# Layer norm ahead of the experts taken by token, expert weights centred on the chip, and a reordered end of the program

## The chip, the cores and the metric

The kernel runs on one core of a Trainium2 chip. The metric is the device time of one execution in microseconds (us); less is better. The engines are named as in the profile: PE is TensorE, DVE is VectorE, ACT is ScalarE, POOL is GpSimd, SP is SyncE, whose queue issues most DMAs.

## The reference

Four sequences (batches) of 256 tokens, width 128, go through four residual steps. `ctx` is a context of 4 x 1601 tokens. All is float32.

```python
x = x + xattn0(layernorm(x), ctx)          # 16 heads of 8, rotary, bias by distance, gate
x = x + tanh(layernorm(x) @ W1 @ W2 @ W3 + b)
x = x + xattn1(layernorm(x), ctx, mask)    # 16 heads of 8
x = x + experts(layernorm(x))
...
def experts(x):                            # E = 8 experts, K = 2
    scores = maximum(x @ gate_W + gate_b, 1e-4)
    p = softmax(scores)
    w = maximum(p, 0.1); w = w / (sum of w over the two largest p)
    comb = where(one of the two largest, w, 0)
    y = einsum('bsd,edf->bsef', x, expert_W) + expert_b
    return einsum('bsef,bse->bsf', y, comb) / 2
```

## The kernel before, in words

**Stages and units.** The program has NJ = 8 stages j. Stages 0 to 3 do the first attention for batches 0 to 3, stages 4 to 7 the second. A stage has UB = 52 units: 13 tiles of 124 (the last 113) context tokens times 4 groups of 4 heads. For each unit PE makes the scores (L414, in the first attention also a bias, L408) into two PSUM banks, ACT takes their exponential (L941), and PE multiplies that by the values (L430), accumulating in banks ACC and ACC+1. The loop goes by pairs of units: PE issues the scores of the next pair, then `beside(j, 2 * pair)`, then the values of this pair, then `beside(j, 2 * pair + 1)`.

**Slots.** `beside(j, slot)` holds all other PE work: it is placed by slot numbers, 0 to 51 in a stage. Slot 3 picks the attention's sums of the stage before (`pick`); `gate_at` places the steps that end a batch of the first attention, `expert_at` those of the experts. In stages 5, 6 and 7 the nine steps of `experts(j - 5, k)` stand at slots 8, 10, 11, 13, 14, 24, 25, 27 and 30; for the last batch they follow the last stage. Work in an even slot stands ahead of the values of its pair, work in an odd slot behind them.

**Side banks.** All of this side work shares two PSUM banks, LOW = 6 and HIGH = 7. `fill(bank, ...)` numbers every filling and makes PE wait until DVE or ACT has read the filling before (`seen`); PE's queue is in order, so such a wait also holds the scores and values behind it.

**The end of an attention.** `copy_sums(j)` (L1268) takes the sums out of PSUM. `pick(j)` (L442) brings numerators into LOW and denominators into HIGH, `take_sums` (L1273) copies them, and `finish` tests the denominators, takes their reciprocal (L1282), multiplies (L1285, which raises `batch_done`), tests the result and reduces the tests into `checks` (L1290). `decide()` reduces all `checks` to the flag `redo`, which decides at the end of the program whether everything is computed again in a safe way.

**The norm ahead of the experts** works with features on partitions. `project` adds the attention's output to x (L1362); PE takes the mean (L466); DVE subtracts it and squares (L1310, L1312); PE sums the squares (L472); DVE adds eps (L1316); POOL raises to the power -0.5 (L870); PE spreads the result over the partitions (L479); DVE multiplies (L1321). Then PE makes the gate scores (L523), `choose` (L1375 to L1411, 18 small DVE instructions with one ACT exponential, L956, among them) makes the factors `comb`, PE turns them (L530), makes x plus the experts' biases (L536, L538) into LOW, and makes the experts' products for 128 tokens at a time, four experts into LOW and four into HIGH (L545). `weigh` adds each product times its factor to y (L1427, 16 instructions of 128 x 128 per batch). One `dma_start` per 128 tokens stores y (L728).

**Other queues.** `query_parts(b)` splits the second attention's queries into three bf16 parts on DVE (L1355, L1357) and POOL. POOL norms the context of batch 3 (`norm_context`, L835) after `query_parts(0)`; PE's keys of batch 3 (L352, stage 2, slot 7) wait for that. In stage 1 `fold_weights` fills LOW at slot 4 and HIGH at slot 5, `turn_rstd` fills HIGH at slot 6 of stages 1 and 2. SP's queue stores and places keys in order of the program; ACT's `second_keys` (L967) waits for such a store before it overwrites its buffer.

## Time and profile before

| | before |
|---|---|
| median of 3 runs | 655.69 us (654.56 to 656.54) |
| the profiled execution, its own time | 653.17 us |
| its span, first to last instruction | 651.4 us |
| mean granted TensorE clock | 0.939 |
| PE, DVE, ACT, POOL busy | 86%, 43%, 66%, 22% of the span |

The stages begin (start of their first exponential) at 42.55, 149.20, 234.08, 317.92, 379.95, 435.59, 493.85 and 551.99 us; the last exponential ends at 609.7 us. The span is what the profile's rows lie in; the execution's own time is 1.8 us more. An engine's idle time costs something only where another engine on the path waits for it, so each part of the program is to be read by which wait ends last in it. "[0.52 <-PE ps L414]" behind a row says that its engine was idle for 0.52 us before it, and what ended that.

### The profile page before, as it was taken

How to read it: one execution, taken by the hardware profiler on the slowest of the kernel's cores; microseconds unless marked ns; L12 is line 12 of the kernel's file. 1: busy time of each engine (PE TensorE's matmuls, PEld its weight loads, DVE VectorE, ACT ScalarE, POOL GpSimd, SP SyncE). 2: the span in 40 equal slices, each digit the busy share in tenths (PEclk: the TensorE clock that was granted, in tenths of full speed). 3: DMA queues.
4: the chain of work that ended last, by engine and by line, in shares of the span. 5: the costliest groups of instructions: out<-in, count | busy, mean ns of one | idle time of the engine just before them, and what ended most of it. 6: DMA issues, size and time to landing. Idle time of an engine off the chain costs nothing.

```text
span 651.4 us, 15145 instructions
## 1 busy us (share of the span) xinstructions
PE 561.3 (86%) x6326; PEld 278.2 (43%) x6326; DVE 277.1 (43%) x711; ACT 431.1 (66%) x486; POOL 142.4 (22%) x149
## 2 busy tenths in 40 slices
PE   4665896999979996999999999999999999999643
PEld 3432453545434553445555445434443443443231
DVE  5732742483754424544242243134344343433333
ACT  1224554866747773777778897998789869888400
POOL 5552622354436003541011000100000000000000
PEclk9867997999979997999999999999999999999856
DMA  6366264438755700445370066039016501000000
GB/s 166 94 186 178 71 218 168 104 115 243 226 157 146 264 26 5 138 130 179 83 189 28 27 147 141 27 82 230 4 46 144 133 10 53 2 1 10 1 0 12
DMA packets 54185, 68.12 MB, mean 105 GB/s; under 512 B 13347, under 2 KB 45551, under 8 KB 54112
## 3 DMA queue, kind: packets, MB, share of 16 engines
q1 hardware_dynamic: 50528, 59.29, 32.8%
q0 software_dynamic: 1280, 6.56, 3.4%
q10 hardware_dynamic: 2304, 1.25, 0.7%
q8 instruction: 51, 0.84, 0.5%
q14 instruction: 22, 0.18, 0.1%
HBM read 35.20 MB, written 18.83 MB: 83 GB/s over the span
## 4 chain that ended last, share of the span: by engine, by line
PE 53%; issue 14%; ACT 10%; SPq 7%; DMA 7%; DVE 7%; POOL 1%; ACTq 0%; POOLq 0%; DVEq 0%
PE ps L430 19%; PE ps L414 10%; ACT probs L941 8%; PE ps L408 7%; DMA k_scratch<-k_parts 4%; PE ps L360 4%; SPq L676 2%; PE ps L545 2%; SPq L699 1%; DMA ctx_tokens<-in_ctx 1%; PE ps L352 1%; PE ps L479 1%; PE ps L466 1%; DMA mask_q<-in_mask 1%; PE ps L472 1%
## 5 line engine op out<-in xcount | busy, mean ns | idle before, releaser
L941 ACT ACTIVATE probs<-ps 124x1024 f32<-124x1024 f32 (+1 forms) x416 | 399.8, 1024 | 110.7 <-PE ps L414 109.0
L430 PE MATMUL ps<-probs,values 124*9 124x256 f32 (+1 forms) x3328 | 221.4, 384 | 1.4 <-DVE out_sums L1268 1.3
L414 PE MATMUL ps<-q_side,k_side 63*124 63x256 bf16 (+1 forms) x1664 | 164.5, 283 | 13.0 <-ACT probs L941 11.2
L414 PEld LDWEIGHTS ps<-q_side,k_side 63*124 63x124 bf16 (+1 forms) x1664 | 98.1, 133 | 88.4 <-ACT probs L941 58.7
L430 PEld LDWEIGHTS ps<-probs,values 124*9 124x9 f32 (+1 forms) x3328 | 71.0, 90 | 94.1 <-issue 40.5
L408 PE MATMUL ps<-bias_g,bias_w 64*124 64x512 bf16 (+1 forms) x416 | 88.0, 419 | 25.5 <-ACT probs L941 22.0
L408 PEld LDWEIGHTS ps<-bias_g,bias_w 64*124 64x124 bf16 (+1 forms) x416 | 28.1, 131 | 69.3 <-ACT probs L941 45.3
L870 POOL TENSOR_TENSOR post_rstd<-post_rstd,power 128x2 f32<-128x2 f32 x12 | 8.4, 704 | 167.0 <-DVE post_rstd L1316 167.0
L967 ACT ACTIVATE k<-ps,columns_sb 128x496 f32<-128x496 f32 (+2 forms) x16 | 9.5, 594 | 48.2 <-PE ps L354 30.4
L1188 DVE SCALAR_TENSOR_TENSOR k_swapped<-ps,beta_products,k_sin_sb 32x496 f32<-32x496 f32 (+2 forms) x64 | 40.4, 631 | 0.9
L829 POOL DMA_DIRECT2D mask_q<-in_mask x16 | 9.1, 570 | 141.4 <-DVE checks L1247 141.4
L1254 DVE TENSOR_REDUCE sample_max<-ps 128x8 f32<-128x512 f32 x32 | 20.6, 686 | 41.3 <-PE ps L377 41.3
L1230 DVE TENSOR_TENSOR values<-ps,rstd 124x256 f32<-124x256 f32 (+2 forms) x32 | 12.0, 374 | 60.6 <-PE ps L360 60.5
L360 PE MATMUL ps<-w_centred,ctx_turned 128*124 128x256 f32 (+1 forms) x104 | 32.9, 439 | 4.8 <-ACT k_parts L968 2.5
L1427 DVE SCALAR_TENSOR_TENSOR y<-ps,comb,y 128x128 f32<-128x128 f32 x64 | 22.4, 351 | 16.7 <-PE ps L545 14.7
L360 PEld LDWEIGHTS ps<-w_centred,ctx_turned 128*124 128x124 f32 (+1 forms) x104 | 18.6, 202 | 16.4 <-issue 8.0
L1247 DVE TENSOR_REDUCE checks<-mask_q 128x1 f32<-128x801 int32 (+1 forms) x16 | 15.6, 977 | 23.0 <-DMA mask_q<-in_mask 22.9
L855 POOL TENSOR_TENSOR k<-k,k_parts 128x496 f32<-128x496 f32 (+2 forms) x16 | 15.1, 944 | 42.0 <-ACT k_parts L968 41.9
L352 PE MATMUL ps<-ctx_normed,w_centred 128*128 128x496 f32 (+2 forms) x32 | 16.9, 613 | 8.3 <-POOL ctx_normed L835 5.7
L859 POOL TENSOR_TENSOR k<-k,k_parts 128x496 f32<-128x496 f32 (+2 forms) x16 | 15.1, 944 | 29.5 <-DVE k_parts L1199 28.3
L1268 DVE COPY out_sums<-ps 128x512 f32<-128x512 f32 x16 | 10.6, 686 | 23.6 <-PE ps L430 23.6
L545 PE MATMUL ps<-expert_w_sb,xn 128*128 128x512 f32 x32 | 18.8, 718 | 0.6 <-DVE y L1420 0.6
(190 smaller groups left out, 481.6 us busy)
## 6 DMA issues: line engine op xcount, KB each, us to landing
k_side<-k_scratch SPq DMA_DIRECT2D x24, 400.2 KB, 9.0
k_side<-k_parts SPq DMA_DIRECT2D x48, 124.0 KB, 2.4
k_scratch<-k_parts SPq DMA_DIRECT2D x16, 372.0 KB, 4.1
v_scratch<-values SPq DMA_DIRECT2D x4, 936.0 KB, 8.1
values<-v_scratch SPq DMA_DIRECT2D x4, 936.0 KB, 14.4
v_scratch<-v SPq DMA_DIRECT2D x12, 288.0 KB, 3.4
mask_q<-in_mask POOLq DMA_DIRECT2D x8, 400.5 KB, 3.9
mask_q<-in_mask POOLq DMA_DIRECT2D x8, 400.0 KB, 3.5
```

The lines of the kernel that those rows point to most:

```text
L352: pe.matmul(ps[:, LOW, 0:w], w0c[:, 2, :], cn[:, k_0:k_1], start=True, stop=True).then_inc(made[LOW], 1)
L360: last = pe.matmul(ps[0:r, bank, 2 * D * i:2 * D * i + 2 * D], ct[:, TS * t:TS * t + r], wvv.rearrange("p l d -> p (l d)"), start=True, st ...
L408: pe.matmul(ps[0:width, bank, :], G["bias_w"][rows, at], G["bias_g"][rows, t:t + 1, :].broadcast_to((HALF, 2, SQ)), start=True, stop=False ...
L414: last = pe.matmul(ps[0:width, bank, SQ * i:SQ * (i + 1)], kst[rows, j % 2, 2 * g + i, at], qst[rows, j % 2, 2 * g + i, :], start=not bias ...
L430: last = pe.matmul(ps[32 * i:32 * i + VC, ACC + g // 2, SQ * (g % 2):SQ * (g % 2) + SQ], v[0:rows, j % 2, t, h, :], p[0:rows, u % 4, SQ * ...
L545: pe.matmul(ps[:, bank, :], xn[:, b * SQ + 128 * t:b * SQ + 128 * t + 128], ew[:, 4 * i:4 * i + 4, :].rearrange("p e d -> p (e d)"), start ...
L855: pool.tensor_tensor(k1[:, s, 0:w], k1[:, s, 0:w], kp1[:, s, 0, 0:w], ALU.subtract).then_inc(rest1, 1)
L941: act.activation(p[0:rows, u % 4, :], ps[0:rows, s:s + 2, :].rearrange("p a n -> p (a n)"), ACT.Exp)\
L1188: last = dve.scalar_tensor_tensor(out=kb[to:to + 32, 0:w], in0=ps[at:at + 32, LOW, 0:w], scalar=beta_cols[at:at + 32, 2:3], in1=k_sin[at:a ...
L1247: dve.tensor_reduce(checks[:, at:at + 1], mask_q[:, 0:k_1 - k_0], AX.X, ALU.min, apply_absolute_value=True)\
L1254: dve.tensor_reduce(mx[:, c, H8 * half_:H8 * half_ + H8], ps[:, bank, :].rearrange("p (h k) -> p h k", k=SAMPLE), AX.X, ALU.max).then_inc( ...
L1427: add = dve.scalar_tensor_tensor(out=out[:, t, :], in0=ps[:, bank, D * i:D * i + D], scalar=comb[:, t, e:e + 1], in1=out[:, t, :], op0=ALU ...
```

## The change

1. **By token.** `project` only adds. Step 1 of the experts transposes x with a matmul against the identity into HIGH and multiplies x by the gate weights into LOW, both without a norm before them. `token_norm` takes mean and variance along the free axis (`bn_stats`, `bn_aggr`), POOL raises to the power, and the result, one number per token, is a factor on the gate scores and on `comb` (`comb_rstd`). The copy of the transposed x is y's start; the mean, sum of squares, spread and normed x are gone. 
2. **Centred weights.** Since the products take x and not x less its mean, `centre_experts` multiplies gate and expert weights by the centring matrix once, at slot 24 of stage 4: three matmuls on PE, three copies on DVE.
3. **Slots.** Six steps in place of nine, at slots 8, 10, 22, 24, 26 and 29. The gate's exponential on ACT stands 7 units behind slot 10 (before: 7 behind slot 14).
4. **End of each attention.** `take_sums` takes the reciprocal of the denominators directly from PSUM, copies them, and multiplies the numerators from PSUM; the tests (`check_sums`) come after. LOW and HIGH are released later, `batch_done` is raised earlier.
5. **End of the program.** The last batch's products are made ahead of `comb`, for both halves of the tokens, into banks 0 to 3. DVE weighs the first half in 8 steps; ACT scales the second half's 8 products, and DVE adds them in three halving steps and one more. `check_sums` stands between `token_norm` and `choose`, `decide` last.
6. `w_scaled` lies in a part of `probs` and no longer in a tile of its own.

```diff
+CENTRE_EXPERTS_AT = (NB, 24)
 def expert_at(j, slot):
-    steps = (8, 10, 11, 13, 14, 24, 25, 27, 30)
+    steps = (8, 10, 22, 24, 26, 29)
...
-        GATE_STEPS = 17
+        GATE_STEPS = 18
...
+            def centre_experts():
+                pe.wait_ge(expert_in, 16 * N_EXPERT)
+                fill(LOW, "gate_w")
+                pe.matmul(ps[:, LOW, 0:E], centre[:], gw[:], start=True, stop=True).then_inc(made[LOW], 1)
+                for i, bank in enumerate((HIGH, LOW)):
+                    fill(bank, "expert_w", i)
+                    pe.matmul(ps[:, bank, :], centre[:], ew[:, 4 * i:4 * i + 4, :].rearrange("p e d -> p (e d)"), start=True, stop=True)\
+                      .then_inc(made[bank], 1)
...
                 elif k == 1:
                     pe.wait_ge(seen[LOW], side.of(LOW, "o1", b))
-                    post_mean(HIGH, ("mean", norm), b)
-                elif k == 2:
-                    post_var(LOW, ("var", norm), norm)
-                elif k == 3:
-                    post_spread(HIGH, ("spread", norm), norm)
-                elif k == 4:
-                    pe.wait_ge(seen[HIGH], side.of(HIGH, "spread", norm))
...
+                    fill(HIGH, "xt", b)
+                    for t in range(TT):
+                        last = pe.matmul(ps[:, HIGH, 128 * t:128 * t + 128], x[:, b * SQ + 128 * t:b * SQ + 128 * t + 128], ident[:],
+                                         start=True, stop=True)
+                    last.then_inc(made[HIGH], 1)
+                    pe.wait_ge(gw_centred, 1)
                     fill(LOW, "gate", b)
...
             pick(NJ - 1)
-            for k in range(4):
+            for k in range(2):
+                experts(NB - 1, k)
+            for t in range(TT):
+                expert(NB - 1, t, (2 * t, 2 * t + 1))
+            for k in (2, 3):
                 experts(NB - 1, k)
             pe.wait_ge(least_ready, 1)
-            fill(LOW, "least")
-            pe.transpose(ps[0:1, LOW, 0:128], least[:], ident[:]).then_inc(made[LOW], 1)
-            for k in range(4, 9):
-                experts(NB - 1, k)
+            fill(HIGH, "least")
+            pe.transpose(ps[0:1, HIGH, 0:128], least[:], ident[:]).then_inc(made[HIGH], 1)
...
             def take_sums(j):
-                for out, bank in ((num, LOW), (den, HIGH)):
-                    dve.wait_ge(made[bank], side.of(bank, "pick", j))
-                    dve.tensor_copy(out[:], ps[:, bank, 0:SQ]).then_inc(seen[bank], 1)
+                dve.wait_ge(made[HIGH], side.of(HIGH, "pick", j))
+                dve.reciprocal(inv[:], ps[:, HIGH, 0:SQ]).then_inc(den_ready, 1)
+                dve.tensor_copy(den[:], ps[:, HIGH, 0:SQ]).then_inc(seen[HIGH], 1)
+                dve.wait_ge(made[LOW], side.of(LOW, "pick", j))
+                dve.wait_ge(den_ready, j + 1)
+                dve.tensor_tensor(att[:, columns(j % NB)], ps[:, LOW, 0:SQ], inv[:], ALU.mult).then_inc(seen[LOW], 1)
+                dve.wait_ge(seen[LOW], side.of(LOW, "pick", j))
+                dve.sem_inc(batch_done, 1)
...
+            def token_norm(b):
+                dve.wait_ge(made[HIGH], side.of(HIGH, "xt", b))
+                for t in range(TT):
+                    dve.bn_stats(est[:, t, :], ps[:, HIGH, 128 * t:128 * t + 128]).then_inc(e_stats, 1)
+                dve.wait_ge(e_stats, TT * (b + 1))
+                for t in range(TT):
+                    dve.bn_aggr(emv[:, t, :], est[:, t, :]).then_inc(e_aggr, 1)
+                dve.wait_ge(e_aggr, TT * (b + 1))
+                dve.tensor_scalar(prs[:], emv[:, :, 1], EPS, None, ALU.add).then_inc(e_var, 1)
...
+                dve.tensor_copy(y[:, b % 2], ps[:, HIGH, 0:SQ].rearrange("p (t d) -> p t d", d=D)).then_inc(seen[HIGH], 1)
...
+            def weigh_last():
...
+                for e in range(E):
+                    dve.wait_ge(last_made, 1 + e // 4)
+                    dve.scalar_tensor_tensor(out=out[:, 0, :], in0=ps[:, e // 4, D * (e % 4):D * (e % 4) + D], scalar=comb_r[:, 0, e:e + 1],
+                                             in1=out[:, 0, :], op0=ALU.mult, op1=ALU.add).then_inc(y_done if e == E - 1 else last_sum, 1)
...
+                for i, n in enumerate((4 * D, 2 * D, D)):
+                    dve.tensor_tensor(weighed[:, 0:n], weighed[:, 0:n], weighed[:, n:2 * n], ALU.add).then_inc(last_sum, 1)
+                    dve.wait_ge(last_sum, E + i)
+                dve.tensor_tensor(out[:, 1, :], out[:, 1, :], weighed[:, 0:D], ALU.add).then_inc(y_done, 1)
...
             take_sums(NJ - 1)
-            finish(NJ - 1)
             project(NB - 1)
+            token_norm(NB - 1)
+            check_sums(NJ - 1)
+            choose(NB - 1)
+            weigh_last()
             decide()
-            choose(NB - 1)
-            weigh(NB - 1)
```

Where the order of the work moves, it is shown here as the program issues it, before and now.

PE, the end of the program (behind the last values), before:

```order
924 L442 MATMUL ps<-out_sums,pick 32x256 x8
925 L510 MATMUL ps<-att,L_wo_sb 128x256
926 L466 MATMUL ps<-x,ones_mean 128x256
927 L472 MATMUL ps<-ones_mean,post 128x1 x2
928 L479 MATMUL ps<-ident,post_rstd 128x128 x2
929 L620 MATMUL ps<-ident,least 1x128
930 L523 MATMUL ps<-gate_w_sb,xn 128x8 x2
931 L530 MATMUL ps<-ident,comb 8x128 x2
932 L536 MATMUL ps<-ident,x 128x128
933 L538 MATMUL ps<-expert_b_sb,comb_t 128x128
936 L545 MATMUL ps<-expert_w_sb,xn 128x512 x4
```

and now:

```order
911 L449 MATMUL ps<-out_sums,pick 32x256 x8
912 L532 MATMUL ps<-att,L_wo_sb 128x256
913 L537 MATMUL ps<-ident,x 128x128 x2
914 L543 MATMUL ps<-gate_w_sb,x 128x8 x2
915 L523 MATMUL ps<-expert_w_sb,x 128x512 x4
916 L550 MATMUL ps<-ident,comb 8x128 x2
917 L556 MATMUL ps<-expert_b_sb,comb_t 128x128 x2
918 L640 MATMUL ps<-ident,least 1x128
```

The four products (x4) now stand ahead of the turned factors, the norm's three steps are gone, and the flag's transpose is last.

DVE, stage 2 behind the copies of the attention's sums, up to the query parts (`CAST`) for which POOL waits, before:

```order
201 L1273 COPY num<-ps 128x256
202 L1273 COPY den<-ps 128x256
203 L1170 COPY rstd<-ps 124x13
204 L1277 TENSOR_SCALAR inside<-den 128x256
205 L1279 SCALAR_TENSOR_TENSOR inside<-den,inside 128x256
206 L1282 RECIPROCAL den<-den 128x256
207 L1285 TENSOR_TENSOR att<-num,den 128x256
208 L1287 SCALAR_TENSOR_TENSOR inside<-att,inside 128x256
209 L1290 TENSOR_REDUCE checks<-inside 128x1
210 L1355 CAST q_parts<-post 128x256
211 L1357 CAST q_parts<-post 128x256
```

and now:

```order
200 L1298 RECIPROCAL inverse<-ps 128x256
201 L1299 COPY den<-ps 128x256
202 L1302 TENSOR_TENSOR att<-ps,inverse 128x256
203 L1196 COPY rstd<-ps 124x13
204 L1308 TENSOR_SCALAR inside<-den 128x256
205 L1310 SCALAR_TENSOR_TENSOR inside<-den,inside 128x256
206 L1313 SCALAR_TENSOR_TENSOR inside<-att,inside 128x256
207 L1316 TENSOR_REDUCE checks<-inside 128x1
208 L1381 CAST q_parts<-post 128x256
209 L1383 CAST q_parts<-post 128x256
```

Reciprocal and product now stand ahead of the copy of `rstd` (which waits for PE's step at slot 6), the tests behind it.

## Rows read from the trace of the kernel before

**Rows 1.** The page, part 1: busy us, share of the span, instructions

```profile
PE 561.3 (86%) x6326; PEld 278.2 (43%) x6326; DVE 277.1 (43%) x711; ACT 431.1 (66%) x486; POOL 142.4 (22%) x149
```

**Rows 2.** Stretches: us, busy us (count) of PE, PEld, DVE, ACT, POOL, granted clock, DMA share, GB/s

```profile
541.00:575.00 34.00, 32.06 (x434) 14.49 (x426) 11.15 (x23) 31.02 (x34) 1.26 (x2) 1.00 0.05 14
251.00:255.00 4.00, 3.75 (x24) 2.38 (x28) 1.72 (x5) 2.06 (x4) 4.00 (x5) 0.50 0.02 4
638.40:640.80 2.40, 2.40 (x4) 1.01 (x4) 1.62 (x5) 0.00 (x0) 0.00 (x0) 0.50 0.00 0
```

**Rows 3.** Timeline of the end: start us, us, engine line op tiles [idle before]

```profile
611.16 1.07 PE L442 MATMUL ps<-out_sums,pick 128*32 128x256 f32 x16 [0.81 <-DVE out_sums L1268]
...
612.30 0.42 DVE L1273 COPY den<-ps 128x256 f32<-128x256 f32 x1
612.76 0.29 DVE L1277 TENSOR_SCALAR inside<-den 128x256 bf16<-128x256 f32 x1
...
613.55 1.75 DVE L1282 RECIPROCAL den<-den 128x256 f32<-128x256 f32 x1
...
615.82 1.22 PE L510 MATMUL ps<-att,L_wo_sb 128*128 128x256 f32 x2 [3.58 <-DVE att L1285]
...
617.08 0.48 DVE L1362 SCALAR_TENSOR_TENSOR x<-ps,folded_bias,x 128x256 f32<-128x256 f32 x1 [0.40 <-PE ps L510]
...
621.85 1.22 PE L479 MATMUL ps<-ident,post_rstd 128*128 128x128 f32 x4 [1.02 <-POOL post_rstd L870]
...
624.51 1.00 PE L523 MATMUL ps<-gate_w_sb,xn 128*128 128x8 f32 x4 [0.46 <-DVE lowest L1441]
625.54 0.17 DVE L1375 TENSOR_TENSOR gate_scores<-ps,gate_b_sb 128x16 f32<-128x16 f32 x1 [1.00 <-PE ps L523]
...
630.00 0.59 PE L530 MATMUL ps<-ident,comb 128*8 128x128 f32 x2 [4.49 <-DVE comb L1411]
...
631.82 0.79 PE L538 MATMUL ps<-expert_b_sb,comb_t 8*128 8x128 f32 x2
...
634.64 6.91 PE L545 MATMUL ps<-expert_w_sb,xn 128*128 128x512 f32 x8 [0.59 <-DVE y L1420]
...
640.58 3.06 DVE L1427 SCALAR_TENSOR_TENSOR y<-ps,comb,y 128x128 f32<-128x128 f32 x8 [0.54 <-PE ps L545]
```

**Rows 4.** The statistics of x's tokens near the program's start: ns min/median/max

```profile
L1058 DVE BATCH_NORM_STATS2 x_stats<-out_sums x8: 275/278/289, 5.0 to 66.4; 128x6 f32<-128x128 f32 x8
```

**Rows 5.** Timeline of stage 6: exponentials behind side work, and the side work

```profile
506.63 1.94 ACT L941 ACTIVATE probs<-ps 124x1024 f32<-124x1024 f32 x2 [0.52 <-PE ps L414]
509.42 1.94 ACT L941 ACTIVATE probs<-ps 124x1024 f32<-124x1024 f32 x2 [0.85 <-PE ps L414]
511.62 1.94 ACT L941 ACTIVATE probs<-ps 124x1024 f32<-124x1024 f32 x2 [0.26 <-PE ps L414]
513.76 3.77 ACT L941 ACTIVATE probs<-ps 124x1024 f32<-124x1024 f32 x4 [0.21 <-PE ps L414]
517.39 0.24 ACT L956 ACTIVATE gate_p<-gate_scores 128x16 f32<-128x16 f32 x1
...
525.19 1.94 ACT L941 ACTIVATE probs<-ps 124x1024 f32<-124x1024 f32 x2 [1.87 <-PE ps L414]
...
526.27 1.98 PE L545 MATMUL ps<-expert_w_sb,xn 128*128 128x512 f32 x4
...
528.66 3.77 ACT L941 ACTIVATE probs<-ps 124x1024 f32<-124x1024 f32 x4 [1.54 <-PE ps L414]
534.38 3.77 ACT L941 ACTIVATE probs<-ps 124x1024 f32<-124x1024 f32 x4 [1.95 <-PE ps L414]
```

**Rows 6.** Timelines of stages 1 and 2

```profile
186.04 0.67 ACT L967 ACTIVATE k<-ps,columns_sb 128x496 f32<-128x496 f32 x1 [3.96 <-DMA k_scratch<-k_parts]
...
244.65 0.17 DVE L1170 COPY rstd<-ps 124x13 f32<-124x13 f32 x1 [2.96 <-PE ps L344]
...
251.25 0.79 PE L352 MATMUL ps<-ctx_normed,w_centred 128*128 128x124 f32 x2 [5.66 <-POOL ctx_normed L835]
```

129 lines of the change are left out of this document (81 added, 48 removed).

## The prediction

> **What bounds the kernel now.** I first read part 1 of the page [rows 1]: PE is busy for 86% of the span, ACT for 66%. That says where to look and not what anything is worth, so I went on by stretches [rows 2]: in an undisturbed part of the last stages PE is busy for 32.06 of 34 us and ACT for 31.02, at the full clock (2.4 GHz). Both are nearly full, so PE work beside the units turns up as idle time of ACT. The timeline of stage 6 shows that [rows 5]: seven of its idle gaps lie behind the experts' steps, 0.52, 0.85, 0.26, 0.21, 1.87, 1.54 and 1.95 us, together 7.20 us. The third view is the timeline behind the last exponential [rows 3]. There only one thing happens at a time: from PE's pick at 611.16 to the end of the last weighing step at 643.64 each row begins where another ends, for 32.5 us, and every saved wait is saved time. PE runs there at half rate (1.2 GHz), still in 638.40 to 640.80 [rows 2]; before the clock fell it had gone idle with the last scores. The last view is the timelines of stages 1 and 2 [rows 6], for what the change to `take_sums` meets: in stage 2 PE stands 5.66 us for POOL's normed context, which waits for DVE.
>
> **The end of the program**, step by step, from the same 611.16 us [rows 3]. Denominators are picked at 611.16 + 1.07 = 612.23. Reciprocal 1.75, copy 0.42 and product 0.42, with some 0.2 of gaps, raise `batch_done` in time for PE at 615.05 (before 615.82): 0.8 won, since three tests and a copy no longer stand ahead. PE's output step to DVE's start takes 617.08 - 615.82 = 1.26, DVE's addition 0.48, a gap 0.06: 616.85. Then, in place of mean, square, variance, power, spread and multiply (each a PE or DVE step of its own, up to the gate's matmuls at 624.51), comes the transposed x, four matmul instructions like the spread's, 1.26 to DVE's start: 618.11. Statistics twice 0.28 [rows 4]; aggregates and the addition of eps at most 0.5 (three small instructions, each no longer than the 0.17 of such rows): 619.2. POOL's power now runs beside DVE's copy to y and the four tests: 0.42 + 0.29 + 0.43 + 0.42 + 0.42 and gaps, 2.2 us, and these decide: `choose` starts at 621.4. It ended, with PE's next start, 630.00 - 625.54 = 4.46 later; one more small instruction makes 4.6: factors at 626.0. Meanwhile PE has made the gate's scores (1.0, to 619.1) and the products, 6.91, to 626.05: both arrive together. Turning the factors 0.6, their copy 0.42 as for any 256 elements, the biases two of the four matmuls, 1.5 at half rate, to 628.65. DVE adds them, 0.45, weighs eight products, 3.06 + 0.05, to 632.2. The second half is ACT's: a scaled copy of 128 x 128 can't take less than the 0.24 of its smallest row [rows 5], and I allow 0.5, so at most 4 us from 626.2, ready by 630.2, under DVE's eight. Four additions of 512, 256, 128 and 128 elements: the 256-element rows take 0.42, the others scaled by it 0.7, 0.29 and 0.29, with gaps 1.85: 634.05 against 643.64. **9.6 us saved.** The flag, 1.1 us of work moved behind it, lies beside the storing of y, which took from 643.64 to the end of the span at 651.4 with what follows; if nothing covered it, it would cost 1.1.
>
> The half rate may end sooner. PE now works without a gap from 616.85 to 626.05, 9.2 us; before, some 9 us of biases and products (631.82 to 640.80) passed and the clock was still at half at their end. So the rise would meet only the last steps: turned factors and biases, 2.1 us at half rate, half of that at most saved. Between 0 and 1.1 I take **0.5**.
>
> **Stages 5 to 7.** I price steps by the idle gap they left in ACT [rows 5], not by their own length. The output step stays (0.52). Transposed x and gate stand in one pair, as mean and variance did: 0.85 again. The spread's and the old gate's slots are empty: 0.26 + 0.21 saved. The pair with turned factors and four matmuls for x and biases left 1.87; now the factors stand alone (0.2, as the short steps did) and two matmuls two slots on (0.5). The products [rows 5] left 1.54 and 1.95; in an even and an odd slot with work in the pair before, 1.62 and 1.54. Sum now 0.52 + 0.85 + 0.2 + 0.5 + 1.62 + 1.54 = 5.2 against 7.2: 2.0 a stage, **5.9 us** for three. The centring adds, in stage 4, two products of the same 512 columns in an even slot, 1.95, and a small one: **2.1 us lost.** Net 3.8. Bounds: if only the two empty slots help, 3 x 0.47 - 2.1 = 0.7 is lost; if the new slots hid the biases and factors whole, 3 x 2.7 - 2.1 = 6.0 is won. I stay near the middle, since every step has a row of its kind.
>
> What makes this hold is that nobody waits for the factors. ACT's small exponential started at 517.39, behind 21 units; now it stands four units sooner, near 513.0. The scores will be ready for it by then: slot 10's work lies ahead of the exponential at 509.42, transposed x is there by 507.4; 1.1 to the statistics' end, POOL's power 0.9 at most, DVE's small steps 0.9, 510.3. The factors follow 3.5 us later, 516.5. Slot 22 lies 12 units behind slot 10 (506.7), at 1.05 us a unit 519.2. The slack is 2.7 us.
>
> **`take_sums` in the other stages.** In stage 2 DVE stood idle for 2.96 us between its two copies and the copy of `rstd` [rows 6]; reciprocal and product now fill that, and the query parts come 1.75 + 0.42 + gaps = 2.2 us sooner. POOL and PE's keys (251.25) wait for just that, so PE starts at 249.0. But the clock was at half there [rows 2], after 5.66 us of idle PE, and PE was full (3.75 of 4 us). If it stays at half as long, work started 2.2 us sooner is worth half: **1.1 us**; 0 if another wait takes over, 4 if the shorter wait spares the fall. In stage 1 the same edit costs: LOW is released 1.8 us later than `fold_weights` at slot 4 wants it, and PE's queue stands. I cost this at nothing, because ACT later waits 3.96 us for a store of keys at 186.04 [rows 6], a chain through SP's queue of stores that this PE work doesn't feed; without that cover it is 1.8. In stages 3 to 7 `batch_done` comes sooner, but PE had no wait of note there: nothing. `w_scaled` within `probs` moves nothing.
>
> One price has no row: a reciprocal that reads PSUM. The row from SBUF says 1.75 for 256 elements, 7 ns each; a copy from PSUM takes 0.42 and a scalar test from SBUF 0.29 [rows 3], so the source makes 0.13 of difference there. The lower end is 1.75, the upper 3.5 (twice), and I take 1.75, since 7 ns per element is far above the 1.6 of the copy.
>
> The Trainium skill has a rule against this edit ("VectorE: DVE Perf Modes", "Why PSUM operands drop a tier"): an operand in PSUM excludes the mode in which both SBUF read ports serve one tensor. The rows of copy and test agree in kind. For the reciprocal the rule would give up to the doubled time, the second rival below.
>
> **Sum.** 9.6 + 0.5 + 3.8 + 1.1 = 15.0 us. The profiled execution took 653.17, so 638.2 for its like; it lay 2.5 below the median of the runs shown, 655.69, and against that I forecast **640.7**.
>
> **The rivals.**
> - *The gaps don't close* (0.10). The slots move the work but PE is as full, and stage 1's stall isn't covered: the stages give nothing, -1.8 beside: 9.6 + 0.5 + 1.1 - 1.8 = 9.4, so 646.3. For it: PE busy 94% there. Against: ACT's gaps follow PE's side work row by row.
> - *The reciprocal from PSUM is twice as long* (0.08). 1.75 more at the end; in stage 2 it overruns DVE's idle time by 1.0: 15.0 - 2.8 = 12.2, so 643.5. Against: 7 ns per element.
> - *The clock is kinder* (0.09). It doesn't fall in stage 2 (3 more) and rises early at the end (0.6 more): 18.6, so 637.1. For it: PE's wait in stage 2 shrinks to 3.5 us.
> - *Slower* (0.03). The factors come too late for slot 22 in each of stages 5 to 7: PE stands ahead of the values, ACT runs dry and the clock falls to half as it did in stage 2. With 5 us of wait and 6 us at half rate (3 lost) that is 8 a stage, 24 in all: 655.7 - 15.0 + 24 = 664.7. It turns the sign once the wait costs over 5 us a stage, that is, when ACT's exponential or POOL's power comes 4 to 8 us later than worked out above. Against: 2.7 us of slack.
> - *No change* (0.02): the stored y or the flag sets the end and the stages lose what they gain, 655.7.
>
> **How the numbers follow.** The forecast's own case has 0.68. About 2 us (0.3%) is what a measurement of this kernel tells from no change. All cases but the last two are faster: 0.95, same 0.02, slower 0.03. The range: from between the forecast and the kind clock, 636.0, to between the doubled reciprocal and the first rival, 645.5; that leaves out the first rival and the last two, 0.15, and a little of the others.
>
> **What would show it right or wrong.** At the end: the reciprocal from PSUM near 1.75 us; `choose` starting some 10 us behind the pick and waiting for nothing; products ending as the factors arrive; the last addition some 23 us behind the pick (before 32.5). ACT's idle time in stages 5 to 7 near 6.4 us each, in stage 4 some 2 us more than before. PE's wait for the normed context near 3.5 us. Wrong would be a wait of PE for the factors at slot 22, an exponential of the gate behind an idle ACT, a stage 1 that is 2 us longer, or ACT's scaled copies ending after DVE's eighth step.

## The result, and the profile after

| | before | changed |
|---|---|---|
| median (lowest to highest of 4 runs each) | 655.82 us (654.56 to 656.54) | 637.00 us (634.12 to 637.61) |
| ratio | | 0.971, 95% interval 0.967 to 0.974 |
| the profiled execution, and its span | 653.17, 651.4 us | 636.57, 634.5 us |
| mean granted TensorE clock | 0.939 | 0.942 |

The change saves 18.8 us, 3.7 us more than the 15.0 that were forecast; 640.7 was predicted, and 637.0 lies 1.0 us inside the range's lower end, 636.0.

Where it went is read stage by stage. A stage's length is the time from its first exponential to that of the next stage (of stage 7, to the end of its last exponential); "start" is the first exponential of all, "end" runs from the start of PE's last pick to the end of the last instruction that adds to y. The second column is a further profile of the kernel before, the last one of a further run of the changed kernel (both are among the experiments).

| us | before | before, again | changed | changed, again |
|---|---|---|---|---|
| start | 42.55 | 43.49 | 42.47 | 42.84 |
| stage 0 | 106.65 | 109.93 | 108.80 | 109.33 |
| stage 1 | 84.89 | 85.39 | 84.32 | 83.31 |
| stage 2 | 83.83 | 83.96 | 82.61 | 82.07 |
| stage 3 | 62.03 | 62.03 | 62.02 | 62.03 |
| stage 4 | 55.64 | 55.64 | 57.78 | 57.78 |
| stages 5, 6, 7 | 58.26, 58.13, 57.69 | 58.33, 58.13, 57.69 | 55.95, 55.82, 55.24 | 55.98, 55.82, 55.24 |
| end | 32.48 | 31.79 | 20.40 | 20.49 |

By the first profile of each, the end gave 12.1, stages 5 to 7 gave 7.1, stage 2 gave 1.2, stage 1 0.6, and stage 4 took 2.1: 18.9 together. Stage 0, which the change does not touch, came out 2.1 us longer in this one profile. Stages 0 and 1 vary by some 3 us from profile to profile, whatever the kernel; that is why the two profiled executions lie only 16.6 us apart and the medians 18.8. Both stages wait for stores of keys, and their length goes with the time that the clock is at half rate in them (experiment 8). Stages 3 to 7 repeat to 0.2 us, so one profile is enough there.

The page, part 1 (busy us, share of the span, instructions), against [rows 1]:

```profile
PE 549.7 (87%) x6292; PEld 271.3 (43%) x6292; DVE 272.1 (43%) x718; ACT 433.1 (68%) x494; POOL 142.4 (22%) x149
```

PE lost 11.6 us of work and its share of the span rose. The shares say nothing of the gain; the stretches do. Stretches of the changed kernel (us, then busy us and count of PE, PEld, DVE, ACT, POOL, granted clock, DMA share, GB/s), the first of them in stage 2, the rest at the end of the program:

```profile
251.00:255.00 4.00, 4.00 (x32) 2.04 (x31) 1.72 (x5) 2.56 (x4) 3.78 (x5) 0.50 0.01 4
606.50:611.50 5.00, 1.84 (x19) 0.82 (x20) 2.85 (x4) 0.00 (x0) 0.00 (x0) 1.00 0.00 0
611.50:618.30 6.80, 6.80 (x15) 3.70 (x16) 5.01 (x22) 0.22 (x1) 0.69 (x1) 0.50 0.01 4
618.30:621.70 3.40, 2.13 (x9) 0.82 (x7) 1.99 (x11) 1.52 (x7) 0.00 (x0) 0.99 0.00 0
```

In stage 2 the clock still fell to half (1.2 GHz), as in [rows 2]. At the end it fell 5.0 us behind the pick, over the transposed x and the products, and was full again (2.4 GHz) from 618.3. Before, it had fallen 2.3 us behind the pick and stayed down for 27.3 us, until 640.8, so for all of PE's steps but the last 0.75 us of the products.

The timeline of the end (start us, us, engine line operation tiles, idle before and what ended it), against [rows 3]:

```profile
606.50 1.07 PE L449 MATMUL ps<-out_sums,pick 128*32 128x256 f32 x16 [0.81 <-DVE out_sums L1294]
607.63 1.76 DVE L1298 RECIPROCAL inverse<-ps 128x256 f32<-128x256 f32 x1 [1.19 <-PE ps L449]
...
610.14 0.67 PE L532 MATMUL ps<-att,L_wo_sb 128*128 128x256 f32 x2 [2.58 <-DVEq L1304]
...
611.39 1.14 PE L537 MATMUL ps<-ident,x 128*128 128x128 f32 x4 [0.58 <-DVE x L1388]
...
612.57 0.49 DVE L1395 BATCH_NORM_STATS2 e_stats<-ps 128x6 f32<-128x128 f32 x2 [1.23 <-PE ps L537]
613.03 6.31 PE L523 MATMUL ps<-expert_w_sb,x 128*128 128x512 f32 x8
613.10 0.25 DVE L1398 BATCH_NORM_AGGREGATE e_mean_var<-e_stats 128x2 f32<-128x6 f32 x2
...
613.63 0.69 POOL L891 TENSOR_TENSOR post_rstd<-post_rstd,power 128x2 f32<-128x2 f32 x1 [48.45 <-DVE post_rstd L1400]
...
615.36 0.35 DVE L1424 SCALAR_TENSOR_TENSOR gate_scores<-ps,post_rstd,gate_b_sb 128x8 f32<-128x8 f32 x2
...
619.99 0.38 PE L550 MATMUL ps<-ident,comb 128*8 128x128 f32 x2 [0.65 <-DVE comb L1461]
620.18 2.18 ACT L1072 ACTIVATE probs<-ps,comb_rstd 128x128 f32<-128x128 f32 x8 [3.60 <-DVE comb_rstd L1463]
...
620.87 0.71 PE L556 MATMUL ps<-expert_b_sb,comb_t 8*128 8x128 f32 x4 [0.50 <-DVE comb_t L1465]
621.69 0.42 DVE L1471 TENSOR_TENSOR y<-y,ps 128x256 f32<-128x256 f32 x1 [0.87 <-PE ps L556]
622.14 3.06 DVE L1499 SCALAR_TENSOR_TENSOR y<-ps,comb_rstd,y 128x128 f32<-128x128 f32 x8
625.11 1.47 DVE L1506 TENSOR_TENSOR probs<-probs 128x512 f32<-128x512 f32 x3
...
626.61 0.29 DVE L1508 TENSOR_TENSOR y<-y,probs 128x128 f32<-128x128 f32 x1
```

The reader is to see that from 612.57 on DVE goes from step to step, with short waits only for ACT's exponential, the turned factors and the biases: the products, 6.31 us of PE, end at 619.3, ahead of the factors at 619.99, and nobody waits for them. ACT's copies end at 622.4, long before DVE needs them at 625.11. The reciprocal from PSUM took 1.76 us, as from SBUF. The flag, now worked out behind y, is ready 21.4 us behind the pick, and from the last addition to the end of the span it is 7.6 us (before 7.7): its 1.1 us of work is covered.

Stage 6, exponentials behind side work, and the two steps that depend on the gate, against [rows 5]:

```profile
506.73 1.94 ACT L962 ACTIVATE probs<-ps 124x1024 f32<-124x1024 f32 x2 [0.52 <-PE ps L421]
509.28 3.77 ACT L962 ACTIVATE probs<-ps 124x1024 f32<-124x1024 f32 x4 [0.61 <-PE ps L421]
512.91 0.24 ACT L977 ACTIVATE gate_p<-gate_scores 128x16 f32<-128x16 f32 x1
521.01 1.94 ACT L962 ACTIVATE probs<-ps 124x1024 f32<-124x1024 f32 x2 [0.35 <-PE ps L421]
523.21 1.94 ACT L962 ACTIVATE probs<-ps 124x1024 f32<-124x1024 f32 x2 [0.26 <-PE ps L421]
526.73 1.94 ACT L962 ACTIVATE probs<-ps 124x1024 f32<-124x1024 f32 x2 [1.58 <-PE ps L421]
530.20 11.62 ACT L962 ACTIVATE probs<-ps 124x1024 f32<-124x1024 f32 x12 [1.54 <-PE ps L421]
```

```profile
519.24 0.38 PE L550 MATMUL ps<-ident,comb 128*8 128x128 f32 x2
```

Six gaps, together 4.86 us, where seven made 7.20. The gate's exponential starts without an idle ACT ahead of it, at 512.91 (forecast 513.0), and PE turns the factors at 519.24 without a wait.

Stage 2 (DVE's reciprocal and PE's keys), against [rows 6]:

```profile
242.77 1.76 DVE L1298 RECIPROCAL inverse<-ps 128x256 f32<-128x256 f32 x1 [4.41 <-PE ps L449]
...
250.50 0.79 PE L359 MATMUL ps<-ctx_normed,w_centred 128*128 128x124 f32 x2 [3.41 <-POOL ctx_normed L856]
```

PE waits 3.41 us for the normed context and not 5.66, 2.25 less, as forecast (near 3.5).

### The profile page after: what moved, and what is told of

It is laid out like the page before. It is cut to its first block, busy times and chain, and to the rows that moved or that the text cites. A ratio compares the mean times of both kernels' runs of the same rounds, so it can differ in the third digit from the quotient of the medians.

```text
span 634.5 us, 15118 instructions
## 1 busy us (share of the span) xinstructions
PE 549.7 (87%) x6292; PEld 271.3 (43%) x6292; DVE 272.1 (43%) x718; ACT 433.1 (68%) x494; POOL 142.4 (22%) x149
## 4 chain that ended last, share of the span: by engine, by line
PE 59%; ACT 12%; DVE 8%; DMA 8%; issue 7%; SPq 4%; ACTq 0%; POOL 0%; DVEq 0%; POOLq 0%
PE ps L437 22%; PE ps L421 12%; ACT probs L962 10%; PE ps L415 8%; DMA k_scratch<-k_parts 5%; PE ps L367 4%; PE ps L523 2%; SPq L694 2%; PE ps L359 1%; DMA ctx_tokens<-in_ctx 1%; PE ps L361 1%; PE ps L449 1%; DMA mask_q<-in_mask 1%; ACT k_parts L989 1%; DVE k_swapped L1214 1%
## 5 line engine op out<-in xcount | busy, mean ns | idle before, releaser
L415 PE MATMUL ps<-bias_g,bias_w 64*124 64x512 bf16 (+1 forms) x416 | 87.8, 418 | 27.6 <-ACT probs L962 24.1
L367 PE MATMUL ps<-w_centred,ctx_turned 128*124 128x256 f32 (+1 forms) x104 | 34.5, 457 | 3.5 <-ACT k_parts L989 2.1
L1298 DVE RECIPROCAL inverse<-ps 128x256 f32<-128x256 f32 x8 | 14.1, 1758 | 28.6 <-PE ps L449 28.6
L359 PE MATMUL ps<-ctx_normed,w_centred 128*128 128x496 f32 (+2 forms) x32 | 16.6, 603 | 6.5 <-POOL ctx_normed L856 3.4
L1483 DVE SCALAR_TENSOR_TENSOR y<-ps,comb_rstd,y 128x128 f32<-128x128 f32 x48 | 16.8, 351 | 12.4 <-PE ps L523 10.9
```

What stands on the lines that cost most here:

```text
L359: pe.matmul(ps[:, LOW, 0:w], w0c[:, 2, :], cn[:, k_0:k_1], start=True, stop=True).then_inc(made[LOW], 1)
L367: last = pe.matmul(ps[0:r, bank, 2 * D * i:2 * D * i + 2 * D], ct[:, TS * t:TS * t + r], wvv.rearrange("p l d -> p (l d)"), start=True, st ...
L415: pe.matmul(ps[0:width, bank, :], G["bias_w"][rows, at], G["bias_g"][rows, t:t + 1, :].broadcast_to((HALF, 2, SQ)), start=True, stop=False ...
L1483: add = dve.scalar_tensor_tensor(out=out[:, t, :], in0=ps[:, bank, D * i:D * i + D], scalar=comb_r[:, t, e:e + 1], in1=out[:, t, :], op0=A ...
```

## The experiments

Each result is the median with the lowest and highest run, and the ratio to the kernel before on the same chip, with its 95% interval. The first four were made together (before: 654.78 us), the next four together (before: 655.05), the last four together (before: 654.75).

**1. The changed kernel again.** No edit.

> The changed kernel once more. The profile after shows 16.9 us less span than the one before: stages 5 to 7 give 7.1, the end behind the pick 12.1, stage 2 1.2, stage 1 0.6, stage 4 takes 2.1, and stage 0 was 2.1 us longer. Theory A: all but stage 0 is the change's own, and stage 0 varies from run to run, so the median lies 18 to 20 us below the kernel before. Theory B: the 3.7 us beyond the forecast come from a lucky phase of PE's clock in that run; then this comes out 15 to 16 us below. In the profile A wants the end (pick to last addition of y) at 20.4 us, give or take 1 for where the half rate begins; B wants 22 to 23.

636.0 us (633.2 to 638.4), ratio 0.971 (0.968 to 0.974), 18.8 us below the kernel before, and the end is 20.49 us: theory A. The size of the gain holds in a second set of runs, and so do the lengths of stages 2 to 7 (table above).

**2. The end in the old order.** The products go back behind the gate, two banks at a time, and DVE weighs all of them. ACT's half of the weighing goes with the order, so this edit tests the two together.

```diff
-            for k in range(2):
-                experts(NB - 1, k)
-            for t in range(TT):
-                expert(NB - 1, t, (2 * t, 2 * t + 1))
-            for k in (2, 3):
+            for k in range(6):
                 experts(NB - 1, k)
...
-            weigh_last()
+            weigh(NB - 1)
```

> Only the order of the end is undone: the last batch's products come behind the factors and biases, into the side banks, and DVE weighs all 16; the norm by token, the centring, the slots and the sums stay. Theory A (the products' 6.3 us lay beside the choice of experts, and ACT took half of the weighing): from the start of the products to the last step of y is then 9.0 us as before, and this starts 15.2 us behind the pick, 24.2 in place of 20.4, with up to 0.9 more for biases at half rate: 3.8 to 4.7 us slower than the changed kernel. Theory B (the factors were the bound, ACT's help is worth nothing): 1 us slower at most.

641.38 us (640.02 to 644.46), ratio 0.981 (0.978 to 0.984): 5.4 us above the changed kernel. The timeline of its end:

```profile
602.80 1.07 PE L449 MATMUL ps<-out_sums,pick 128*32 128x256 f32 x16 [0.81 <-DVE out_sums L1282]
...
619.79 3.78 PE L523 MATMUL ps<-expert_w_sb,x 128*128 128x512 f32 x4 [0.58 <-DVE y L1459]
...
625.34 3.60 PE L523 MATMUL ps<-expert_w_sb,x 128*128 128x512 f32 x4 [1.76 <-DVE y L1471]
627.49 3.06 DVE L1471 SCALAR_TENSOR_TENSOR y<-ps,comb_rstd,y 128x128 f32<-128x128 f32 x8 [2.30 <-PE ps L523]
```

The last addition ends 27.75 us behind the pick, against 20.4. So 7.3 us of the end hang on the products' place and on ACT's help in this form; the medians show 5.4, and what made up for 1.9 us is not shown. This undo costs more than the old end did: here both banks of a half are filled before either is counted as free, so that PE stands 1.76 us between the halves, and products and weighing took 10.8 us where they took 9.0 before (634.64 to 643.64). Less that 1.8, the changed kernel's end is 5.6 us shorter. Of these 0.6 lie ahead of `choose` (it starts 9.5 us behind the pick here, 8.9 in the changed kernel), where the clock had fallen sooner in this profile; 0.7 are turned factors and biases, at half rate here and at the full clock in the changed kernel; 4.3 are the products' place and ACT's half of the weighing, which no run separates. The other 6.5 of the 12.1 lie between the kernel before and this one, both at half rate: `choose` starts 4.9 us sooner (norm by token, earlier sums), and from there to the products it is 1.6 us less, with two of the four matmuls for x and biases gone. My expectation had left the wait between the halves out.

**3. The new sums alone.** The kernel before with the new `take_sums` and `check_sums`, and `w_scaled` within `probs`; nothing else of the change.

```diff
 def take_sums(j):
-    for out, bank in ((num, LOW), (den, HIGH)):
...
+    dve.reciprocal(inv[:], ps[:, HIGH, 0:SQ]).then_inc(den_ready, 1)
...
```

> The kernel before with the new take_sums and check_sums alone (and w_scaled within probs); at the end the tests follow the sums at once. Theory A: stage 2 is 1.1 to 1.2 us shorter, because POOL's context norm starts sooner and half of that is given back at half rate; stage 1's stall of PE at slot 4 (some 1.8 us) is covered by ACT's wait for the store of keys; the end gains 0.4. Sum 1.6 us faster than before. Theory B (the stall of stage 1 counts): 0 to 0.3 us slower than before, and stage 1 1.8 us longer in the profile.

650.43 us (649.2 to 654.8), ratio 0.995 (0.993 to 0.997), 3.5 to 4.4 us below the kernel before, more than was expected. Its profile:

```profile
250.43 0.79 PE L353 MATMUL ps<-ctx_normed,w_centred 128*128 128x124 f32 x2 [3.41 <-POOL ctx_normed L836]
```

Stage 2 is 82.11 us, 1.7 shorter, with the same 3.41 us of wait as in the changed kernel, and the end is 31.25 us, 0.5 to 1.2 shorter: 2.2 to 2.9 us have a place. Stage 1 measured 84.00, not longer. That is within the spread of stage 1, so the last 1 to 2 us of this median are not accounted for; the interval's lower bound, 2.1 us, is met by what the profile shows.

**4. Without the centring.** Its three matmuls and three copies are left out.

```diff
-                if (j, slot) == CENTRE_EXPERTS_AT:
-                    centre_experts()
```

> The changed kernel without the centring of gate and expert weights (that part of the computation is left out). Theory A: the centring costs stage 4 what one idle gap of ACT shows, 2.1 to 2.2 us, and nothing later: this kernel is 2.1 us faster than the changed one, and stage 4 as long as before (55.6 us). Theory B (later stages had made up for it, or the DVE copies hid it): no difference.

633.89 us (631.88 to 635.78), ratio 0.969 (0.966 to 0.971): 2.1 us below the changed kernel (experiment 1), and stage 4 is 55.65 us where it was 57.78. The stage shows the term to its tenth; the medians alone, with runs that spread over 4 us, would not. The gap that the centring leaves in the changed kernel's ACT is this row,

```profile
414.63 10.70 ACT L962 ACTIVATE probs<-ps 124x1024 f32<-124x1024 f32 x11 [2.17 <-PE ps L421]
```

and there is none at this place without it.

**5. Stage 1's banks free at once.** At the start of stage 1 only, DVE copies both sums first as before and divides after `rstd`'s copy.

```diff
-                take_sums(j - 1)
+                copy_first(0) if j == 1 else take_sums(j - 1)
...
                 copy_turned_rstd(j + 1)
+                if j == 1:
+                    divide(0)
```

> The changed kernel, but in stage 1 alone numerators and denominators are copied out first, as before, and reciprocal and product follow behind the folded weights. PE's stall at slot 4 (3.39 us of ACT idle there against 1.79 before) goes. Theory A (covered by ACT's wait for the store of keys, 20 units later): the gap at slot 4 is 1.8 again, the wait for the store is longer by as much, and the time is that of the changed kernel within 1 us. Theory B (not covered): 1.6 us faster.

637.41 us (633.12 to 640.74), ratio 0.972 (0.968 to 0.975), no difference from the changed kernel. ACT's rows in stage 1 show why; first the changed kernel, then this one:

```profile
165.56 1.94 ACT L962 ACTIVATE probs<-ps 124x1024 f32<-124x1024 f32 x2 [3.39 <-PE ps L421]
...
188.45 0.67 ACT L988 ACTIVATE k<-ps,columns_sb 128x496 f32<-128x496 f32 x1 [3.16 <-DMA k_scratch<-k_parts]
```

```profile
165.60 1.94 ACT L962 ACTIVATE probs<-ps 124x1024 f32<-124x1024 f32 x2 [1.79 <-PE ps L421]
...
190.48 0.67 ACT L988 ACTIVATE k<-ps,columns_sb 128x496 f32<-128x496 f32 x1 [5.16 <-DMA k_scratch<-k_parts]
```

The stall of PE is there, 3.39 against 1.79 us, as costed. Taken away, the 1.6 us come back in front of the store, 5.16 against 3.16; the keys behind the store start 37.6 us into the stage here and 37.2 to 37.8 in three profiles of the changed kernel. The cover named in the prediction holds up to there. Behind it the two differ: the clock is at half for 6.8 us of this stage 1, and the stage takes 85.73 us (experiment 8). The changed kernel was not run on this chip; by the ratios to the kernel before (0.972 here, 0.971, 0.971 and 0.974 there) no difference shows.

**6. The six steps at old slots.** 24, 25, 27 and 30 in place of 22, 24, 26 and 29.

```diff
-    steps = (8, 10, 22, 24, 26, 29)
+    steps = (8, 10, 24, 25, 27, 30)
```

> The changed kernel with its last four steps in the old slots: 8, 10, 24, 25, 27, 30 in place of 8, 10, 22, 24, 26, 29. The work is the same, only two steps fall into one pair and the products into an odd and an even slot. Theory A (what a pair's slack takes in decides): gaps of 0.52, 0.61, 1.1 (factors and biases together), 1.54 and 1.95, sum 5.7 against 4.87, so 0.85 a stage and 2.6 us in all slower than the changed kernel. Theory B (only the amount of work on PE counts): no difference.

638.05 us (636.91 to 639.56), ratio 0.974 (0.971 to 0.977). Stages 5 to 7 are 56.39, 56.33 and 55.89 us, 0.44, 0.51 and 0.65 longer, 1.6 in all where 2.6 was expected. PE's busy time in stage 6 is only 0.1 us more (52.55 against 52.44), so neither theory holds alone. Most of what the stages gained is from the work that is gone, and 1.6 of the 7.1 from where the rest stands.

**7. The tests later.** All of the last attention's tests go behind the gate's factors.

```diff
-            check_sums(NJ - 1)
             choose(NB - 1)
+            check_den(NJ - 1)
             weigh_last()
+            check_att(NJ - 1)
             decide()
```

> The changed kernel, at the end with the four tests out of the way of choose: the two tests of the denominators while DVE waits for the biases' matmuls (0.87 us idle), the other two behind y, ahead of the flag. Theory A (the tests are what choose waits for, POOL's power is done 1.0 us sooner): choose starts 1.0 us sooner, the flag comes 0.1 us sooner to 0.2 us later and stays hidden beside the last store: 0.9 to 1.0 us faster. Theory B (products or flag take over as the bound): 0 to 0.3 faster.

634.43 us (633.01 to 636.44), ratio 0.969 (0.966 to 0.972). The chain now goes over POOL's power and not over DVE's tests:

```profile
610.86 0.69 POOL L891 TENSOR_TENSOR post_rstd<-post_rstd,power 128x2 f32<-128x2 f32 x1 [48.54 <-DVE post_rstd L1406]
611.66 0.36 DVE L1430 SCALAR_TENSOR_TENSOR gate_scores<-ps,post_rstd,gate_b_sb 128x8 f32<-128x8 f32 x2 [0.55 <-POOL post_rstd L891]
...
624.99 0.14 DVE L1523 TENSOR_SCALAR redo<-lowest 1x1 int32<-1x1 f32 x1
```

`choose` starts 8.0 us behind the pick (before this edit 8.9) and the last addition ends at 19.57 (20.40). That is about the 0.9 expected. But the flag, with two tests ahead of it, is ready no sooner, 21.5 against 21.4 us behind the pick, and of the 0.9 only 0.2 to 0.5 are left from pick to the end of the span (27.6 us against 28.0, 27.9 and 27.8 in three profiles of the changed kernel). That the flag holds the end is a guess that fits; no run tests it. The median lies 1.6 us below experiment 1, which ran on another chip: more than the profile can account for, and within the scatter of both.

**8. The kernel before again**, one run.

> The kernel before once more, for its stages. Stage 0 was 106.65 us and stage 1 84.89 in the first profile, against 106.6 to 109.3 and 82.4 to 84.8 in five profiles with other ends. Theory A: both are bound by stores of keys and vary by 1 to 2 us whatever the kernel, and stages 2 to 7 repeat within 0.3 us except for half rate in stage 2. Theory B: stage 1 of the kernel before is always the longest, so the change gains there as well.

657.26 us, span 655.3. It is there for the second column of the table: of its 4.1 us against the first profile, stage 0 made 3.3, start and stage 1 1.4, and the end took 0.7 back.

Theory B of the expectation is not out. Stage 1 is again longer than in the changed kernel, and what goes with that is the time at half rate within the stage. Of all profiles:

| stage 1, us (of it at half rate) | |
|---|---|
| the kernel before | 84.89 (6.8), 85.39 (6.8) |
| the changed kernel | 84.31 (3.4), 83.31 (none), 82.75 (none) |
| experiment 5, old sums in stage 1 | 85.73 (6.8) |
| experiments 2, 3, 4, 6 | 82.44 (3.4), 84.00 (6.8), 84.81 (3.4), 85.09 (3.4) |
| experiments 7, 10, 11, 12 | 82.85, 83.42, 82.87, 83.00 (none in each) |

Without a fall the stage took 82.8 to 83.4 us, with one 84.0 to 85.7 (but 82.44 in experiment 2). Where the sums are copied out first, PE stood idle for 3.4, 3.6 and 4.6 us until 39 to 40 us into the stage, and the clock was at half there for 6.8 us each time. With the new sums PE stood for 2.6 to 3.4 us there in nine profiles, and the clock fell behind that for 3.4 us in three of them and not at all in six; experiments 2 and 3 had no such wait, but a fall at 12 us. So `take_sums` may save a further 1 to 2 us in stage 1 through the clock (an estimate from these lengths). Three profiles against eleven don't prove it, and the medians of experiment 5 don't show it. Stage 0 varies the same way: 106.57 and 106.65 us with 17 and 18 us at half rate, 109.33 to 110.10 with 21 to 22. Which of the two, length or half rate, brings the other there is open.

**9. The changed kernel a third time**, beside the last three.

> The changed kernel again, beside the next three: the reference against which they are read, all four on one chip. Expected 636 to 637.5 us; stages 5 to 7 near 55.9, 55.8 and 55.2, stage 4 57.8, the end (pick to last weighing step) 20.4 us.

637.51 us (635.08 to 639.33), ratio 0.974 (0.971 to 0.978), on another chip than experiment 1; stage 4 57.78, stages 5 to 7 55.91, 55.83 and 55.25, the end 20.49.

**10. Six idle matmuls at the end.** They keep PE busy behind the pick and behind the products; nobody reads them.

```diff
             pick(NJ - 1)
+            for _ in range(3):
+                pe.matmul(ps[:, 3, :], ident[:], ew[:, 0:4, :].rearrange("p e d -> p (e d)"), start=True, stop=True)
...
                 expert(NB - 1, t, (2 * t, 2 * t + 1))
+            for _ in range(3):
+                pe.matmul(ps[:, 4, :], ident[:], ew[:, 0:4, :].rearrange("p e d -> p (e d)"), start=True, stop=True)
```

> Six matmuls whose results nobody reads, three behind the pick and three behind the products of the last batch, so that PE is idle for less of the end. Theory A (the half rate over the products at the end, 6.8 us of it, comes of PE's idle time behind the last scores): the products run at the full clock for part or all of their 6.3 us, and the result comes 0.5 to 1.5 us sooner than the changed kernel (choose and the tests still set when the factors are ready, so not more). Theory B (the clock falls and rises by something else, or the extra matmuls stand in the way of steps on the path): same or up to 1 us slower.

634.61 us (632.9 to 637.02), ratio 0.970 (0.966 to 0.974). Stretches of its end, from the pick to the factors (columns as above), then two rows of its timeline:

```profile
604.27:609.00 4.73, 4.32 (x24) 1.77 (x24) 2.73 (x4) 0.00 (x0) 0.00 (x0) 1.00 0.00 0
609.00:617.30 8.30, 7.17 (x22) 3.47 (x22) 6.50 (x30) 0.22 (x1) 0.69 (x1) 1.00 0.00 1
```

```profile
609.17 0.71 PE L537 MATMUL ps<-ident,x 128*128 128x128 f32 x4 [0.58 <-DVE x L1392]
...
610.08 3.68 PE L523 MATMUL ps<-expert_w_sb,x 128*128 128x512 f32 x8
```

The clock stayed full. The products took 3.68 us and not 6.2 to 6.3, but they were not on the path; only the transposed x was, 0.71 against 1.23 us in experiment 9, and the end went from 20.49 to 19.98. Theory A holds in both its parts: PE's idle time behind the last scores is what brings the fall (both kernels with these matmuls were without it, all twelve other profiles had it), and 0.5 us hung on it, or 1.0 against the ends of 21.0 us in experiments 4 and 6. The medians lie 2.9 us apart, of which the profile shows 0.5 at the end; the intervals overlap, and I count only the 0.5.

**11. Products spread over pairs.** The expectation misnames the slots: the short steps stood at 20 and 22, the four products at 23, 25, 27 and 29. Slots 22 and 23 are one pair, so the first product shared its pair with the biases.

```diff
-    steps = (8, 10, 22, 24, 26, 29)
+    steps = (8, 10, 20, 22, 23, 25, 27, 29)
```

> Each product of 512 columns in a pair of units of its own (slots 20, 22, 25, 27 for four products, 23 and 29 for the short steps), and the centring's two products in two pairs of stage 4. Theory A (side work costs ACT only what exceeds a pair's slack of about 0.6 to 0.9 us; two such products in neighbouring pairs left 1.59 and 1.54, the first alone about 0.5): gaps of stages 5 to 7 fall from 4.87 to about 3.8 us each, stage 4 from 57.8 to about 56.9, together 4.2 us sooner. Theory B (PE's side work is paid in full wherever it stands, since PE is 94% busy): stages as long as in the changed kernel, within 0.3 us.

635.33 us (634.0 to 636.4), ratio 0.969 (0.966 to 0.972), but stage 4 is 57.98 and stages 5 to 7 are 55.95, 55.85 and 55.28: as long as in the changed kernel, within 0.2 us. Theory B holds for them, and the median's 2.2 us cannot come from the edit. ACT's rows of stage 6:

```profile
518.80 1.94 ACT L965 ACTIVATE probs<-ps 124x1024 f32<-124x1024 f32 x2 [0.21 <-PE ps L421]
522.15 1.94 ACT L965 ACTIVATE probs<-ps 124x1024 f32<-124x1024 f32 x2 [1.42 <-PE ps L421]
524.77 1.94 ACT L965 ACTIVATE probs<-ps 124x1024 f32<-124x1024 f32 x2 [0.68 <-PE ps L421]
527.38 1.94 ACT L965 ACTIVATE probs<-ps 124x1024 f32<-124x1024 f32 x2 [0.68 <-PE ps L421]
530.00 11.62 ACT L965 ACTIVATE probs<-ps 124x1024 f32<-124x1024 f32 x12 [0.68 <-PE ps L421]
```

Gaps of 0.26 (biases), 1.58 and 1.54 (products) became one of 1.42, for biases and first product in one pair, and three of 0.68; with the others the sum is 4.79 us against 4.86. What counts here is PE's work of the whole stage. Stage 6 as one stretch, of the kernel before, of the changed one and of this one:

```profile
493.85:551.98 58.13, 54.72 (x708) 24.72 (x708) 23.78 (x60) 49.49 (x53) 1.85 (x3) 1.00 0.35 85
```

```profile
493.95:549.77 55.82, 52.44 (x698) 23.19 (x698) 23.29 (x63) 49.50 (x54) 1.85 (x3) 1.00 0.37 88
```

```profile
493.71:549.56 55.85, 52.67 (x698) 23.06 (x698) 23.27 (x63) 49.61 (x53) 1.85 (x3) 1.00 0.37 88
```

PE's busy time fell by 2.28 us and the stage by 2.31; what PE leaves free in the stage was 3.41 us and is 3.38. Spread out, PE works 0.23 us more and leaves 3.18 free; with the old slots (experiment 6) it leaves 3.78. So PE's work explains the 2.3 us, and the placing moves the rest by some tenths.

**12. All three**: the spread slots, the late tests and the six matmuls.

> The spread slots, the late tests (all but the denominators' copy behind the gate's factors) and the six extra matmuls together. Theory A: the savings lie in different places and add up: 4.2 + 1.6 + 0.5 to 1.5, so 5.5 to 7 us sooner than the changed kernel, near 630. Theory B: only the late tests count, 1.6 us sooner.

634.32 us (633.49 to 634.71), ratio 0.969 (0.966 to 0.971). The end is 19.04 us against 20.49, so late tests and clock do add up (0.9 + 0.5); the stages give nothing, as in experiment 11. All four of its runs lie below all four of the changed kernel on the same chip (635.08 and up). From pick to the end of the span it is 26.9 us against 27.8, so of the 3.2 us between the medians 0.9 have a place. It is the best whole version of these, by about 1 us that is shown.

## Why the prediction was right, and where it was off

**The end of the program** was the right term and was too small: 12.1 us against 9.6 + 0.5. Leg by leg, in us:

| leg | forecast | measured |
|---|---|---|
| pick to the output step | 3.9 | 3.64 |
| to the statistics | 3.1 | 2.43 |
| statistics to `choose` | 3.3 | 2.79 |
| `choose` to the factors on PE | 4.6 | 4.63 |
| factors to DVE's addition | 2.65 | 1.70 |
| addition and eight weighing steps | 3.5 | 3.5 |
| last four additions | 1.85 | 1.70 |

The second and the fifth leg, 1.6 us together, are the clock but for 0.3, and they are two different things. The fifth is the change's doing. With the products ahead of the factors PE works through the half rate early: the clock is full again from 618.3, before the factors (0.38, at 1.2 GHz 0.59 in experiment 2) and the biases (0.71 against 1.22). There, with the products behind them, it stayed at half from 604.8 for 23.9 us. "So the rise would meet only the last steps" was right, but it met all of both and not half. The second leg is chance. My text asked when the clock would rise, and took for granted that it had fallen by the output step. In nine profiles of kernels whose PE does the same up to that step, the fall came between 2.0 and 5.2 us behind the pick. Where it came before the step or with it (experiments 2, 4 and 6), PE took 1.2 us for it, and the end was 21.0 us in experiments 4 and 6. Where it came behind (three profiles of the changed kernel, experiments 5, 7 and 11), PE took 0.67, and the end, but for experiment 7 with its late tests, was 20.2 to 20.5. The output step of experiment 4, where the fall came 3.5 us behind the pick:

```profile
605.07 1.19 PE L532 MATMUL ps<-att,L_wo_sb 128*128 128x256 f32 x2 [2.58 <-DVEq L1302]
```

The two clock terms should have been 0.7 for the change and 0 to 0.6 for chance, where I took 0.5 in all. The other 1.2 us is small errors of size, one way: copy and tests took 1.91 and not 2.2, DVE's steps overlapping by some hundredths each; the two aggregates together took 0.25; the biases were priced at 1.5 where even at half rate they take 1.22; the sums came 0.25 sooner.

**Stages 5 to 7** gave 7.1, not 5.9. Here the method was off. Pricing each step by the gap that it left in ACT gave 2.0 a stage, since gaps depend on what stood in the pairs around them: transposed x and gate left 0.61, not 0.85 [rows 5], the biases 0.26, not 0.5, and the factors 0.35, not 0.2. The sum over the stage is simpler, the busy time of PE that is gone, 2.28 us; in experiment 11 the gaps moved with the slots while their sum did not. Placing still counts for something: in experiment 6, with 0.1 us more of busy time, the stages were 0.5 us longer. And the slack of 2.7 us was real: factors at 516.5 and slot 22 at 519.2 were worked out, PE turned them at 519.24 with no wait.

**The centring** was costed at 2.1 and took 2.14. **Stage 2** was costed at 1.1 and gave 1.2, by the mechanism named: 2.2 us sooner, at half rate. In the other profiles of kernels with the new sums stage 2 gave 1.0 to 1.8 us. **Stage 1's stall** of 1.6 us was rightly covered by the store (experiment 5), but the prediction asked only in stage 2 what a shorter wait does to the clock; in stage 1 it may be worth 1 to 2 us (experiment 8), which stays open. The reciprocal was costed at 1.75 (measured 1.76). The rule quoted from the Trainium skill ("VectorE: DVE Perf Modes", "Why PSUM operands drop a tier") did not decide this: the second rival, built on a doubled reciprocal, is out.

**The rivals.** The kinder clock came nearest in time, 637.1, but most of it, 3.0 of its 3.6 us, is not what happened: in stage 2 the clock fell as before (0.50 in 251 to 255 us), in every profile. At the end it was kinder, by 0.8 us more than I took, part of it by chance; the nearness is luck. The first rival is out by the stage lengths, the slower one by the gate's exponential, which met no idle ACT, and by slot 22 without a wait. The forecast was right in its mechanisms and low in nearly every size. The sum of the errors, 2.0 at the end and 1.2 in the stages, with 0.6 of stage 1, which is within its scatter, is about the 3.7 us.

## What to carry to other kernels

Where one engine is busy for over nine tenths of a stage, price a change there by the busy time it takes from that engine, and don't expect to win more than some tenths by spreading what is left over more slots; crowding it cost 0.5 us a stage here. Where everything waits for everything, at a program's end, work backwards from what nobody has to wait for: products that need no gate can be made while the gate is worked out, and as long as they end first (here by 0.65 us) neither their length nor the clock they run at matters. Read gains of 1 us from the timeline of the part that is touched; medians of four runs differed by 2 us for kernels whose stages agreed to 0.2 (experiments 9 and 11).
